# Token-half order of the first two head pairs' feature jobs in a one-core decoder-layer kernel

## What is computed

```python
h = layernorm(x)                                     # 2048 tokens x 256
q, k, v, beta = split(h @ W_qkvb)                    # 16 heads x (64 + 64 + 64 + 1)
beta = sigmoid(beta)
q = elu(q) + 1;  k = elu(k) + 1                      # the "features"
q = q / q.sum(-1);  k = k / k.sum(-1)
for t in range(8):                                   # per sequence and head, W starts at 0
    delta = beta[t] * (v[t] - W @ k[t])
    W = W + outer(delta, k[t])
    out[t] = W @ q[t]
x = x + layernorm(h + (out / 8) @ W_o)
```

## Time and profile before

| | us |
|---|---|
| median of 3 runs | 1403.52 (1403.32 to 1403.9) |
| the profiled execution's own time | 1400.74 |
| its span, first to last instruction | 1398.9 |
| PE busy in the span | 1339.3 (96%) |
| DVE busy | 1119.4 (80%) |
| ACT busy | 897.3 (64%) |
| POOL busy | 869.6 (62%) |

### The profile page before, as it was taken

How to read it: one execution, slowest core, us unless ns; L and a number is a source line. 1 busy time by engine, 2 the same in 40 slices (tenths; PEclk the granted TensorE clock), 3 DMA queues, 4 the chain that set the end, 5 groups by cost and what they waited for, 6 DMA issues and landing times. The chain is left out here.

```text
span 1398.9 us, 20735 instructions
## 1 busy us (share of the span) xinstructions
PE 1339.3 (96%) x7362; PEld 1101.9 (79%) x7362; DVE 1119.4 (80%) x1722; ACT 897.3 (64%) x1317; POOL 869.6 (62%) x532
## 2 busy tenths in 40 slices
PE   5999999998999899999999999999999999998997
PEld 4788888897888677777777777777777777777997
DVE  6799998958714789898988989899898988985454
ACT  4544434125556578777777877878777777775774
POOL 2211011105322399999989989989989889873453
PEclk9999999999999999999999999999999999998999
DMA  7502023125664688887878888888878878786572
GB/s 225 83 4 69 1 46 113 31 61 206 223 209 179 196 221 207 216 207 192 219 188 209 214 190 211 214 192 207 210 193 212 210 178 210 172 222 251 195 240 74
DMA packets 171970, 241.22 MB, mean 172 GB/s; under 512 B 34035, under 2 KB 77429, under 8 KB 171872
## 3 DMA queue, kind: packets, MB, share of 16 engines
q1 hardware_dynamic: 156720, 210.21, 59.2%
q10 hardware_dynamic: 13104, 23.86, 5.0%
q0 software_dynamic: 2048, 5.90, 1.1%
HBM read 64.79 MB, written 41.32 MB: 76 GB/s over the span
## 5 line engine op out<-in xcount | busy, mean ns | idle before, releaser
L1170 POOL TENSOR_TENSOR xa_pT<-xa_moved,xa_pT 128x1024 fp32r<-128x1024 f32 x246 | 586.1, 2404 | 35.5 <-ACT xa_pT L1675 32.2
L1498 PE MATMUL xa_S<-xa_kT,xa_qT 128*128 128x512 f32 x1536 | 397.5, 407 | 15.4 <-ACT xa_probs L1681 13.7
L1681 ACT ACTIVATE xa_probs<-xa_S,xa_mx_nb_rinv 128x1024 f32<-128x1024 f32 x256 | 286.1, 1118 | 174.6 <-DVE xa_mx_nb_rinv L1290 174.6
L1515 PE MATMUL xa_O<-xa_pT,xa_v 128*128 128x512 f32 x1536 | 374.4, 392 | 1.0 <-DVE xa_pT L1343 1.0
L1498 PEld LDWEIGHTS xa_S<-xa_kT,xa_qT 128*128 128x128 f32 x1536 | 285.9, 189 | 103.4 <-ACT xa_probs L1681 42.2
L1515 PEld LDWEIGHTS xa_O<-xa_pT,xa_v 128*128 128x128 f32 x1536 | 288.0, 188 | 66.4 <-DVE xa_pT L1343 1.4
L1300 DVE STREAM_TRANSPOSE xa_tq<-xa_probs 128x1024 f32<-128x1024 f32 x256 | 316.7, 1237 | 13.9 <-ACT xa_probs L1681 6.2
L1675 ACT ACTIVATE xa_pT<-xa_moved 128x1024 fp32r<-128x1024 f32 x254 | 253.8, 1049 | 5.1 <-DMA xa_moved<-xa_tq 4.9
L1285 DVE TENSOR_REDUCE xa_mx_nb_rinv<-xa_S 128x1 f32<-128x1024 f32 x128 | 155.6, 1215 | 79.6 <-PE xa_S L1498 77.3
L1287 DVE TENSOR_REDUCE xa_mxp<-xa_S 128x1 f32<-128x1024 f32 x128 | 157.5, 1230 | 18.0 <-PE xa_S L1498 18.0
L482 PE MATMUL fw_pp<-fw_hT,fw_wqk 128*128 128x512 f32 x384 | 97.9, 405 | 7.4 <-DVE fw_hT L622 4.5
(11 more groups left out here) (235 smaller groups left out, 1787.6 us busy)
## 6 DMA issues: line engine op xcount, KB each, us to landing
xa_moved<-xa_tq SPq DMA_DIRECT2D x508, 256.0 KB, 4.5
heads_k<-ci_outs SPq DMA_DIRECT2D x32, 256.0 KB, 2.1
heads_v<-ci_outs SPq DMA_DIRECT2D x32, 256.0 KB, 2.3
heads_q<-ci_outs SPq DMA_DIRECT2D x32, 256.0 KB, 2.2
xa_chunk<-heads_v ACTq DMA_DIRECT2D x32, 256.0 KB, 3.7
ex_w1s<-in_L_ffn_w_dram SPq DMA_DIRECT2D x8, 1024.0 KB, 6.9
ex_w2s<-in_L_ffn_w_dram SPq DMA_DIRECT2D x8, 1024.0 KB, 9.4
xa_chunk<-heads_q ACTq DMA_DIRECT2D x31, 256.0 KB, 3.7
```

The costliest lines, as they stand in the source:

```text
L1170: pool.tensor_tensor(quadrants(pT[LO], r), unit_moved(r), quadrants(pT[HI], r).bitcast(F32), ALU.subtract).then_inc(lo_ready, 1)
L1498: last = pe.matmul(S[:, k], qT[a][:, i // GT % 2, q], kT[b][h % 2][:, k * 512:(k + 1) * 512], start=(n == 0), stop=(n == 2))
L1515: last = pe.matmul(O[:], v[a][:, j * P:(j + 1) * P], pT[b][:, r % PRING, k], start=(j == 0 and n == 0), stop=(j == JT - 1 and n == 2))
L1681: act.activation(probs[:, unit % RING], S[:, 2 * u:2 * u + 2].rearrange("p a b -> p (a b)"), ACT.Exp, bias=nb[:, s % 2:s % 2 + 1], scale=S ...
```

## The change

The first eight feature jobs are taken in another order. Pair 1's chunks 0 and 1 come right after pair 0's chunks 0 and 1, and the second half of the tokens follows for both pairs. The units of dot products are laid out anew up to job 10, and the first unit of pair 1 stands behind the two beta jobs. From job 11 on everything is as it was. No instruction is added or removed.

```diff
+        HALF_STEPS = ((0, 0), (0, 1), (1, 0), (1, 1), (0, 2), (0, 3), (1, 2), (1, 3))
+        HALF_GRAMS = {3: [(0, 0)], 4: [(0, 1)], 6: [(0, 2)], 7: [(0, 3), (0, 4)], 8: [(1, 0), (1, 1)],
+                      9: [(1, 2), (1, 3)], 10: [(1, 4), (2, 0)]}
+
+        def step_of(i):
+
+            return HALF_STEPS[i] if i < len(HALF_STEPS) else divmod(i, CHUNKS)
+
+        def formed(hp, q):
+
+            return max(i for i in range(STEPS) if step_of(i)[0] == hp and step_of(i)[1] <= q) + 1
+
         def grams_after(i):
 
+            if i < 11:
+                return HALF_GRAMS.get(i, [])
@@ project, and the same line in DVE's features
-                hp, q = divmod(i, CHUNKS)
+                hp, q = step_of(i)
@@ gram
-                pe.wait_ge(pp_free, hp * CHUNKS + (b - 1) // 8 + 1)
+                pe.wait_ge(pp_free, formed(hp, (b - 1) // 8))
@@ PE's loop over the jobs
                 if i == BETA_JOB:
                     for s in range(BETA_JOBS):
                         project_beta(s)
+                    gram(*grams_after(i)[0])
@@
-                for hp, u in grams_after(i):
+                for hp, u in grams_after(i)[i == BETA_JOB:]:
                     gram(hp, u)
```

## The result

The changed kernel's median is 1408.09 us (1407.5 to 1411.32, 7 runs), against 1403.32 us for the kernel before, measured again beside it (7 runs). The ratio is 1.0044, with a 95% interval of 1.0034 to 1.0054: 4.8 to 7.6 us slower, 6.2 in the middle. The sign was forecast. The size was not: the sum was +4.4 us, and the range ended 5.8 us above the median before. The two medians alone lie 4.8 us apart; the ratio is higher because the seven runs form two clusters, four from 1407.5 to 1408.1 and three from 1410.1 to 1411.3. One cluster lies where the sum was, the other some 3 us above.

The account below looks back on a forecast made before the run. PE, busy 96% of the span, was taken as the bound. Job (3, 0) at 58.05 + 29.6 + 1.58 = 89.2 against 84.85 gave +4.4 us, so 1403.5 + 4.4 = 1407.9 us, range 1405.8 to 1409.3.

Parts of the forecast that it names:

- What bounds the kernel: Whole kernel: PE's idle time and slowed matmuls count; the shift of job (3, 0) carries to the end.
- Step 1: First jobs: PE's 2.93 us wait falls to 0.5, a 0.7 wait follows, the 1.58 us slow-clock loss goes.
- Step 2: Jobs up to units (0, 3) and (0, 4): PE waits about 1.35 us ahead of (1, 2); these units start at 49.0.
- Step 3: First beta job: waits 6.1 us for POOL's qk_low(3), queued behind copies and ready at 58.05.
- The rival in which the low parts are not late: First beta job: starts at 51.9 without the POOL wait; -1.1 us, 1402.4; chance 0.05.
- Step 4: Beta jobs: the clock falls behind the 6.1 us wait, costing 1.58 us, with bounds 0 and 2.9.
- The rival without the fall: Beta jobs: clock stays up or recovers during the wait, so only the wait is lost; +2.8 us, 1406.3; chance 0.12.
- The bound of 2.9 us: Beta jobs: largest clock loss, if both ran at half speed throughout; used in place of 1.58 for the range's end.
- Step 5: From the beta jobs to (3, 0): 29.6 us in place of 27.2, with a new 0.9 us wait ahead of (3, 0).
- The sum: Job (3, 0) begins at 89.2 against 84.85: +4.4 us, giving 1407.9 at the end.
- The third rival: Later stages, cross attention: lateness partly taken up as slow-clock stretches fall otherwise; +2 to +3 us, 1406; chance 0.12.

Follow-up runs that it names:

- before_fill18: Kernel before the change, with 18 extra matmuls of unused result on PE ahead of job (3, 0), a plain delay; ratio 1.0029 (+4.1 us).
- after_look1: The changed kernel, unaltered, one more single execution profiled for its trace; 1406.49 us.
- after_again: The changed kernel once more, unaltered, against the kernel before; ratio 1.0047 (+6.6 us).
- low_early: The changed kernel with POOL's vb_low(2), vb_low(3) and qk_low(3) moved ahead of sums(2), against the kernel before; ratio 1.0009 (+1.3 us).
- before_low_late: Kernel before the change, with POOL's vb_low(3) and qk_low(3) moved behind sums(6), two units later; ratio 1.0038 (+5.3 us).
- fill_wait: The changed kernel with 25 extra matmuls of unused result on PE in its wait ahead of the first beta job; ratio 1.0039 (+5.4 us).
- after: The changed kernel's first profiled execution, unaltered; 1407.95 us.

## Why the prediction was right in sign and short in size

- **What bounds the kernel** held on average in the old order (before_fill18). In single traces of the new order it did not: the stretch behind (3, 0) differs by up to 3.8 us between three traces of the same kernel, on different chips. The new order lost time in cross attention besides: from the first job of the earlier trace rows to the job behind both (488.67 before, 494.62 in the first trace of the changed kernel) it took 16.69 us against 15.70, and 16.69 in after_look1 and 16.00 in after_again, against 15.77, 15.38 and 15.84 in the other traces of the old order. Whether that is the new order's or chance is open.
- **Step 1, the front gains**, held in place and length: waits of 0.54 and 0.68 us, jobs of 3.0 us. It overlooked that part of the executions starts with two slow jobs, 4 of the 17 traces without the matmuls ahead. Then the old order does not pay its 1.58 us at 27 us. A slow start moves the old order's (0, 2) by +1.1 us and shortens it by 1.6, and it moves the new order's unit (0, 3) by +1.5 (50.80 against 49.33). The difference of 2.0 us, in 4 of 17, takes 0.5 us from the gain. This is an estimate from single traces, not measured by itself.
- **Step 2, the middle**, held: 1.36 us ahead of (1, 2), units (0, 3) and (0, 4) at 49.33 (49.0).
- **Step 3, the wait for POOL**, held to 0.1 us (6.06 against 6.1) and was shown from both sides: low_early takes it away, before_low_late puts it into the old order. The strict first in, first out of GpSimd's queue that the Trainium skill states ("TensorE: Matmul & The Clock Gate", section "Architectural detail: the array is 16× 32×32, not 1× 128×128") fits the trace: in the changed kernel `qk_low(3)` ran from 55.90 on, behind the copies, and in low_early, where it stands ahead of them, it was over at 44.85 + 2.33 = 47.18, so its input had long been ready. The rival in which the low parts are not late fell. Its price of -1.1 us was too good as well: low_early, which makes it true by hand, gave +1.3, since the clock fell behind the wait of 2.32 us ahead of the second beta job and at (3, 0).
- **Step 4, the clock at the beta jobs**, held in kind and was somewhat small in size. The first trace has 7.26 us against the 5.72 of fill_wait, 1.5 us more, but the other eight traces of the new order in which that wait was left open have 7.18 to 7.84; the mean of all nine is 7.53, a cost of 1.8 us instead of 1.58. The rival without the fall occurred in none of them. The bound of 2.9 us was worked out wrongly: both beta jobs at half speed throughout would lose 2.9 each, 5.8 together. The upper end of the range, 1409.3, rests on it; with 5.8 it would have been near 1412, above the 1409.7 that the ratio gives.
- **Step 5 is where it failed.** It computed the new wait ahead of (3, 0) rightly (0.9 against 1.02 us) but priced it at its own length. Step 1 had read from one row, 1.55 us at full clock, that waits below that are free of a fall. Behind a unit of thin matmuls 1.02 us was enough in five of seven traces, for 1.6 us each: 1.1 on average. This and the slow start may be what sets the clusters of runs apart; it is not shown, since neither makes 3 us by itself and the runs without a profile can't be looked into.
- **The sum** becomes 4.4 + 1.1 (step 5) + 0.5 (step 1) + 0.2 (step 4) = 6.2 us, against 6.2 and 6.6 measured. That it fits so well is partly luck: it goes by means of few traces, and the later stages scatter by more than any of these terms. The third rival named falls of the clock in cross attention as what might differ. They did differ, but cost the new order up to 1 us more instead of less; they are not in the sum.

## What to carry to other kernels

When work is put into another order on one engine, look for what another engine has queued by hand behind its results: here one line of POOL's order, untouched by the change, cost 6.1 us of wait and 1.5 to 2.1 of clock. Don't price a new short wait of PE by its length alone: here one of 1 us, behind a unit of thin matmuls, brought a loss of 1.6 us more in five of seven traces. One profile shows one outcome of that; runs that spread in two clusters are a sign to take several. And when a bound is worked out from "both jobs at half speed", add up both.

## What the runs showed of the hardware

- The clock fell behind a wait of 1.02 us that followed a unit of 65-column matmuls (five of seven traces) and never behind one of 1.35 to 1.37 us that followed a job of 512-column matmuls (all 14 traces of the new order). The Trainium skill ("TensorE: Matmul & The Clock Gate", section "A second HAM failure mode: psum-queue depth-cycling") tells of a kernel whose clock swings because PE idles briefly and often between groups of matmuls; here the fall came behind a single such wait, of 1.02 us.
- The same program runs its first two jobs in 7.2 to 7.7 us in some executions and in 5.7 in others, behind the same idle time of 10.7 to 10.9 us. In after_again PE did 5 matmuls from 15.9 to 18.0 us, where it did 9 in the first trace, which would fit half the clock; but the windows view has the granted clock at 1.00 in both, so that it is the clock is not shown, nor what decides it.
- After a slow start the old order's wait of 2.81 us ahead of job (0, 2) left that job at 3.02 us, where waits of 2.93 us were followed by 4.60, 4.37 and 4.61. In cross attention, too, waits of 2.82 us were followed by a job of 4.61 us in one trace and of 3.07 in another (after, after_again). Waits of one length are followed by a fall in some executions and not in others.
